# Replacing the split single-pass output product by a plain fp32 product on two row halves of the TensorE array

## The chip, the cores and the metric

The kernel runs on one core of a Trainium2 chip. The time is device microseconds of that core for one launch, as the median of several executions; the kernel before has three. A separate profiled execution supplies the trace.

## The reference

The input x has the shape (4, 4096, 512). The result is x plus two branches, both computed from the layer-normalised x. The attention branch only touches the first 16 tokens of each of the four sequences and is small. The other branch covers all 16,384 tokens and is most of the work:

```python
s = jnp.einsum('btd,dm->btm', x, Win) + bin_           # 512 -> 64
h = jax.nn.relu(s[..., None] * W1 + b1)                # 64 -> 64 x 16
g = jnp.einsum('btmh,mh->btm', h, W2) + b2             # 64 x 16 -> 64
out = jnp.einsum('btm,md->btd', g, Wout) + bout        # 64 -> 512
```

All of it is float32.

## The kernel before

The tokens are cut into N = 16 groups of 1,024. A group is loaded as eight tiles of 128 tokens, 4 MB in all with its store. The tiles b = 0 (token tiles 0 to 3) and b = 1 (4 to 7) live on two halves of the partitions: in G, partitions 0 to 63 hold the 64 values g of one half of the tokens, and partitions 64 to 127 those of the other.

The order is written out by hand. Each engine runs its own in-order program through the same slots t = 0, 1, 2, ...; a group n starts at slot 8n, and step k of it is due at slot 8n + k. Up to five groups overlap, so that once the pipeline is full every slot modulo 8 holds the same work. The steps are:

- `transpose` (L369 to L378, PE, slots 0 to 7): four 128x128 blocks of x into one PSUM bank, `T_ps[k % 2]`; for k < 2 it waits for load half k. `evacuate` (L508, ACT) copies the bank to xT.
- `s_product` (L380, PE, slots 2, 7, 8, 9): two column halves of the array, 64 columns each. `scale_s` (L765, DVE, slot 10) multiplies by the inverse standard deviation and frees the bank for the first `s_product` of the next group, which is due in the same slot (10 = 8 + 2).
- `statistics` and `variance` (L784, L790, DVE), the inverse root on POOL (L842), `spread_rstd` (PE, slot 9), `copy_rstd` (ACT).
- `s_high`, `s_low`, `replicate` (PE, slots 13 and 17), `relu` (ACT, slots 13 to 20) and `sum_h` (L413, PE, slots 19 to 22; four column tiles of 32).
- G: `g_high` (L544, ACT, slot 23) writes the rounded value g_hi and `g_low` (L776, DVE, slot 24) the rest g_lo to the other partition half, both in the float32r format. G's 128 partitions are then g_hi and g_lo of the same tokens.
- `project` (L430, PE, slots 25 to 32): per token tile two accumulating matmuls over 128 rows, with `wout_hi` and with `wout_lo`.
- `add` (L759, DVE, slots 26 to 33): residual plus product, 128x512, one a tile. `add_bias` (POOL, L867) made the residual before.
- The SP queue stores four tiles at a time once they are added, and loads a later group behind each store.

The attention branch is woven between these steps by `reach(side, ...)`, which runs the next piece of `pe_attention`, `act_attention`, `dve_attention` or `pool_attention` at half-slots of its own. It has three rounds of 24 half-slots from half-slot 34 on and ends by slot T_ATT = 56. Until then its products use one of the two product banks (`A_ps = o_ps[1]`), and `project` has the other alone.

In each slot PE runs: transpose, spread_rstd, attention, project, replicate, sum_h, s_product, attention. DVE runs: add, scale_s, s_low, g_low, attention, statistics, variance, attention.

Of the kernel before, what the change touches and what calls it, by code (L numbers as in the profile page):

```python
# [18 lines left out]
def residual_block(nc, x, Wq, bq, Wk, Wv, bv, Wo, bo, lna_w, lnc_w, lnd_w, Wlq, blq, Wlk, blk, Wlv, blv,  # L19
# [32 lines left out]
    with ctx:  # L52
# [8 lines left out]
        def sem(name):  # L61
            return ctx.enter_context(nc.semaphore(name))
# [22 lines left out]
        w2s = sb("w2s", [P, 2, HK, MH])  # L85
        wout_hi = sb("wout_hi", [P, D], F32R)
        wout_lo = sb("wout_lo", [P, D], F32R)
        bias_row = sb("bias_row", [P, D])
        ones_d = sb("ones_d", [P, P])
        T_ps, s_ps, g_ps, o_ps, rep_ps = [ps("T0"), ps("T1")], ps("s"), ps("g"), [ps("op0"), ps("op1")], ps("rep", 2)  # L90


        xa, lna = Hr[0][1][0:RW, 0:D], Hr[0][1][0:RW, D:2 * D]
        wo2, row1 = Hr[0][0][:, 0:D], Hr[0][0][:, D:2 * D]
        w_nat = [o_sb[i // 2][:, (i % 2) * DC * D:(i % 2 + 1) * DC * D].rearrange("p (c i) -> p c i", c=DC) for i in range(4)]
# [41 lines left out]
        att = vn  # L137
        A_ps = o_ps[1]
        banks = [rep_ps[:, 0:D], rep_ps[:, D:2 * D], o_ps[0][:, :]]
        NB = len(banks)  # L140
# [12 lines left out]
        relu_done, g_done = sem("relu_done"), sem("g_done")  # L153
        hi_done, lo_done = sem("hi_done"), sem("lo_done")
        op_done, xc_done, add_done = sem("op_done"), sem("xc_done"), sem("add_done")
# [9 lines left out]
        turned, turn_dve, turn_act = sem("turned"), sem("turn_dve"), sem("turn_act")  # L165
        spread_made, relu_made, w2s_made, bias_made, wout_made = (
            sem(n) for n in ("spread_made", "relu_made", "w2s_made", "bias_made", "wout_made"))
        qk_ps, qkn_made, v_ps, vn_made, qkT_ps, qkT_made, vT_ps, vT_made = (
# [30 lines left out]

        def product_bank(n, j):  # L200

            t = SLOTS * n + PROJECT + j
            return o_ps[0 if t < T_ATT else j % 2][:, :]

# [13 lines left out]
        def store(n, h):  # L218
            m = n % RING
            sp.wait_ge(add_done, SLOTS * n + 4 * (h + 1))  # L220
            c = slice(h * HALF, (h + 1) * HALF)
            sp.dma_start(out_v[n, :, c], o_sb[m][:, c]).then_inc(st[m][h], 16)

        def sp_program():
# [7 lines left out]
            sp.dma_start(wo2[0:M, :], Wout).then_inc(in_wo2, 16)  # L232
            sp.dma_start(wo2[M:P, :], Wout).then_inc(in_wo2, 16)
            sp.dma_start(bias_row[:, :], bout.partition_broadcast(P)).then_inc(in_rows, 16)
# [156 lines left out]
        def spread_rstd(n):  # L391
            pe.wait_ge(rstd_done, 2 * n + 2)
            if n > 1:
                pe.wait_ge(lo_done, 2 * (n - 1))
            for j in range(4):
                mm = pe.transpose(g_ps[:, j * P:(j + 1) * P], rwide[:, j, :, :].rearrange("p b m -> p (b m)"), ident[:, :])  # L396
            mm.then_inc(rb_done, 1)
# [15 lines left out]
        def sum_h(n, k):  # L413
            pe.wait_ge(relu_done, SLOTS * n + HK + k + 1)
            if k == 0:
                if n == 0:
                    pe.wait_ge(w2s_made, 1)
                if n == N - 1:
                    pe.wait_ge(lo_done, 2 * n)
                else:  # L420
                    pe.wait_ge(R_done, n + 2)
# [8 lines left out]
        def project(n, j):  # L430
            m, t = n % RING, SLOTS * n + PROJECT + j
            if j == 0:
                if n == 0:
                    pe.wait_ge(wout_made, 1)
                pe.wait_ge(lo_done, 2 * n + 2)
            if t >= T_ATT:
                if t <= T_ATT + 1:
                    pe.wait_ge(att_made, 1)
                pe.wait_ge(add_done, SLOTS * n + j - 1)
            elif SLOTS * n + j > 0:  # L440
                pe.wait_ge(add_done, SLOTS * n + j)
            for part in (wout_hi, wout_lo):
                mm = pe.matmul(product_bank(n, j), G[m][:, j * P:(j + 1) * P], part[:, :], start=(part is wout_hi), stop=(part is wout_lo))  # L443
            mm.then_inc(op_done, 1)

        def pe_program():
            pe.wait_ge(ident_made, 1)
            side = [0, pe_attention()]
            for t in range(SLOTS * BODIES):
# [4 lines left out]
                reach(side, 2 * t)  # L454
                if at := due(t, PROJECT, SLOTS):
                    project(*at)
# [51 lines left out]
        def evacuate(n, k):  # L508
            c, b = divmod(k, 2)
            act.wait_ge(tr_done, SLOTS * n + k + 1)  # L510
            if n > 0:
                act.wait_ge(sc_done, 4 * (n - 1) + c + 1)
            act.activation(xT[:, c, b * BLK:(b + 1) * BLK], T_ps[k % 2][:, :], ACT.Copy).then_inc(ev_done, 1)  # L513

# [14 lines left out]
        def relu(n, r):  # L529
            half, k = divmod(r, HK)  # L530
            if k == 0:
                if n == 0:
                    act.wait_ge(xn_made, 1)
                    act.wait_ge(relu_made, 1)
                    act.wait_ge(wout_made, 1)
                    act.wait_ge(bias_made, 1)
                act.wait_ge(rep_done, 2 * n + half + 1)
# [5 lines left out]

        def g_high(n):  # L544
            m = n % RING
            if n == 0:
                act.wait_ge(in_ffn, 16 * 12)
            act.wait_ge(g_done, HK * n + HK)
            for b in range(2):
                own, _, cols = halves(b)  # L550
                act.activation(G[m][own, cols], g_ps[own, :], ACT.Identity, bias=b2c[own, 0:1]).then_inc(hi_done, 1)  # L551

        def act_program():
# [12 lines left out]
            for t in range(SLOTS * BODIES):  # L566
# [6 lines left out]
                reach(side, 2 * t)  # L573
                if at := due(t, G_HIGH):
                    g_high(at[0])
                if at := due(t, RELU, 2 * HK):
# [4 lines left out]
        def dve_attention():  # L581
# [57 lines left out]
            yield 17  # L639
            dve.wait_ge(in_wo2, 32)  # L640
            v = tick(dve.tensor_copy(wout_hi[:, :], wo2))
            dve.wait_ge(in_rows, 32)
            dve.tensor_tensor(bias_row[:, :], bias_row[:, :], row1, ALU.add).then_inc(bias_made, 1)
            dve.wait_ge(dve_own, v)
            dve.tensor_tensor(wout_lo[:, :], wo2, wout_hi[:, :].bitcast(F32), ALU.subtract).then_inc(wout_made, 1)

# [129 lines left out]
        def g_low(n):  # L776
            m = n % RING
            for b in range(2):
                own, other, cols = halves(b)
                dve.wait_ge(hi_done, 2 * n + b + 1)  # L780
                dve.scalar_tensor_tensor(G[m][other, cols], g_ps[own, :], b2c[own, 0:1], G[m][own, cols].bitcast(F32),  # L781
                                         ALU.add, ALU.subtract).then_inc(lo_done, 1)

# [16 lines left out]
        def dve_program():  # L800
            side = [0, dve_attention()]
            for t in range(SLOTS * BODIES):
                if at := due(t, ADD, SLOTS):
# [5 lines left out]
                if at := due(t, G_LOW):  # L809
                    g_low(at[0])  # L810
                reach(side, 2 * t)
# [26 lines left out]
        def inv_std(n):  # L838
            pool.wait_ge(var_done, n + 1)
            if n > 0:  # L840
                pool.wait_ge(rb_done, n)
            pool.tensor_tensor(rstd[:, :], veps[:, :], nhalf[:, 0:TPP], ALU.pow).then_inc(rstd_done, 1)  # L842
            pool.wait_ge(rstd_done, 2 * n + 1)
            pool.tensor_tensor(rwide[:, :, :, :], rstd[:, :].rearrange("p (b j) -> p j b", b=2).unsqueeze(3)
                               .to_broadcast([P, TPP // 2, 2, M]),
# [120 lines left out]
```

## Time and profile before

| | |
|---|---|
| median of 3 runs | 374.67 us (374.19 to 376.34) |
| the profiled execution's own time | 375.8 us |
| its span in the trace | 373.7 us |
| PE busy | 337.0 us (90%) |
| DVE, ACT, POOL busy | 282.9, 278.2, 237.3 us (76, 74, 64%) |

The span is what the trace shows between the first and the last instruction; 2.1 us of the execution's own time lie around it. Busy time of PE comes from matmul records that overlap, so the distance between starts tells more than the durations.

### The profile page before, as it was taken

What the parts mean: (1) busy time and instruction counts of PE and PEld (TensorE: products, weight loads), DVE (VectorE), ACT (ScalarE), POOL (GpSimd) and SP (SyncE); (2) the same over time, 40 slices, a digit from 0 to 9 for tenths busy, and PEclk for the clock granted to TensorE, in tenths of its full rate; (3) what the DMA queues carried; (4) which work ended last, traced back from release to release, by engine and by line L of the source; (5) the groups of instructions that cost most, each with busy time, mean ns of one, the idle gap of its engine ahead of it and who ended that gap; (6) DMA issues with size and microseconds to landing.
All of it is one profiled execution on the core that took longest, in us unless ns stands there. A gap on an engine that the chain in (4) does not pass through costs nothing.

```text
span 373.7 us, 5638 instructions
## 1 busy us (share of the span) xinstructions
PE 337.0 (90%) x1964; PEld 161.1 (43%) x1964; DVE 282.9 (76%) x507; ACT 278.2 (74%) x366; POOL 237.3 (64%) x209
## 2 busy tenths in 40 slices
PE   2489889789997998898999999999999999999774
PEld 2274554345533553444444444444434444443322
DVE  0677757888788799987969687877878787877664
ACT  0363568785786677867998999998989898988820
POOL 8405385992767649839094949494949585769900
PEclk9999989999999999999999999999999999999998
DMA  8999303334346425653575757576756652223647
GB/s 254 266 383 348 117 3 113 112 114 125 157 168 227 153 100 198 224 170 128 216 275 205 263 205 269 203 260 224 280 211 249 224 224 114 113 114 140 208 157 296
DMA packets 15052, 73.02 MB, mean 195 GB/s; under 512 B 4121, under 2 KB 4273, under 8 KB 6833
## 3 DMA queue, kind: packets, MB, share of 16 engines
q1 hardware_dynamic: 12304, 72.23, 53.1%
q0 software_dynamic: 640, 0.16, 0.8%
q10 hardware_dynamic: 2080, 0.28, 0.8%
q8 instruction: 16, 0.26, 0.3%
q14 instruction: 12, 0.09, 0.1%
HBM read 38.96 MB, written 33.69 MB: 194 GB/s over the span
## 4 chain that ended last, share of the span: by engine, by line
PE 63%; POOL 10%; DVE 8%; ACT 6%; issue 5%; DMA 5%; SPq 1%; POOLq 0%; DVEq 0%; ACTq 0%
PE op L443 14%; PE T L377 14%; PE g L425 13%; PE s L387 12%; POOL o L867 7%; DMA o<-in_L_attn_Wv_dram 5%; PE rep L410 4%; ACT H L541 3%; DVE stats L788 2%; PE g L396 1%; POOL rstd L842 1%; DVE o L763 1%; ACT G L551 1%; PE op L276 1%; DVE SH L774 1%
## 5 line engine op out<-in xcount | busy, mean ns | idle before, releaser
L867 POOL TENSOR_TENSOR o<-x,bias_row 128x512 f32<-128x512 f32 x128 | 164.1, 1319 | 4.0 <-issue 4.0
L541 ACT ACTIVATE H<-rep,b1c,w1c 128x1024 f32<-128x1024 f32 x128 | 153.6, 1206 | 14.5 <-PE rep L410 13.7
L763 DVE TENSOR_TENSOR o<-o,op 128x512 f32<-128x512 f32 x128 | 86.9, 682 | 39.3 <-PE op L443 38.3
L513 ACT ACTIVATE xT<-T 128x512 f32<-128x512 f32 x128 | 76.2, 596 | 39.7 <-PE T L377 39.2
L377 PEld LDWEIGHTS T<-ident,x 128*128 128x128 f32 x512 | 54.9, 142 | 107.4 <-issue 75.9
L377 PE MATMUL T<-ident,x 128*128 128x128 f32 x512 | 84.9, 289 | 11.6 <-DMA x<-in_L_attn_x_dram 9.1
L788 DVE BATCH_NORM_STATS2 stats<-x 128x6 f32<-128x512 f32 x128 | 83.2, 682 | 0.4
L842 POOL TENSOR_TENSOR rstd<-veps,nhalf 128x8 f32<-128x8 f32 x16 | 26.4, 1651 | 83.9 <-DVE veps L798 83.9
L387 PE MATMUL s<-xT,win 128*64 128x512 f32 x256 | 70.5, 630 | 0.0
L425 PE MATMUL g<-H,w2s 128*32 128x512 f32 x512 | 68.2, 605 | 0.4 <-ACT H L541 0.4
L443 PE MATMUL op<-wout_hi,G 128*128 128x512 f32 x128 | 62.7, 490 | 5.9 <-DVE G L781 3.7
L443 PE MATMUL op<-wout_lo,G 128*128 128x512 f32 x128 | 51.5, 403 | 0.0
L443 PEld LDWEIGHTS op<-wout_hi,G 128*128 128x128 f32 x128 | 24.5, 192 | 21.1 <-DVE o L763 13.6
L443 PEld LDWEIGHTS op<-wout_lo,G 128*128 128x128 f32 x128 | 24.9, 195 | 0.3
L781 DVE SCALAR_TENSOR_TENSOR G<-g,b2c,G 64x512 fp32r<-64x512 f32 x32 | 24.0, 749 | 1.1
L774 DVE TENSOR_TENSOR SH<-s_full,SH 64x512 fp32r<-64x512 f32 x32 | 23.3, 728 | 2.0 <-ACT SH L527 1.0
L551 ACT ACTIVATE G<-g,b2c 64x512 fp32r<-64x512 f32 x32 | 21.7, 678 | 3.7 <-PE g L425 3.3
L387 PEld LDWEIGHTS s<-xT,win 128*64 128x64 f32 x256 | 13.0, 137 | 22.1 <-issue 18.7
L410 PE MATMUL rep<-SH,spread 128*128 128x512 f32 x64 | 21.5, 417 | 0.7 <-ACT H L541 0.5
L768 DVE TENSOR_TENSOR s_full<-s,s_full 128x512 f32<-128x512 f32 x16 | 11.1, 692 | 14.4 <-PE s L387 14.4
L527 ACT ACTIVATE SH<-s_full 64x512 fp32r<-64x512 f32 x32 | 20.0, 625 | 0.4
L425 PEld LDWEIGHTS g<-H,w2s 128*32 128x32 f32 x512 | 10.1, 108 | 23.1 <-issue 21.5
(166 smaller groups left out, 246.5 us busy)
## 6 DMA issues: line engine op xcount, KB each, us to landing
x<-in_L_attn_x_dram SPq DMA_DIRECT2D x32, 1024.0 KB, 6.8
out_dram<-o SPq DMA_DIRECT2D x32, 1024.0 KB, 4.3
o<-in_L_attn_Wq_dram SPq DMA_DIRECT2D x1, 1024.0 KB, 14.6
o<-in_L_attn_Wk_dram SPq DMA_DIRECT2D x1, 1024.0 KB, 16.4
o<-in_L_attn_Wv_dram SPq DMA_DIRECT2D x1, 1024.0 KB, 19.4
o<-in_L_attn_Wo_dram SPq DMA_DIRECT2D x1, 1024.0 KB, 19.2
H<-in_L_ffn_Wout_dram SPq DMA_DIRECT2D x2, 128.0 KB, 14.7
bias_row<-in_L_ffn_bout_dram SPq DMA_DIRECT2D x1, 256.0 KB, 12.1
```

The costliest lines, as they stand in the source:

```text
L377: mm = pe.transpose(T_ps[k % 2][:, j * P:(j + 1) * P], x_sb[m][:, col0:col0 + P], ident[:, :])
L387: mm = pe.matmul(s_ps[b * M:(b + 1) * M, :], win[:, c, :], xT[:, c, b * BLK:(b + 1) * BLK], start=(c == 0), stop=(c == DC - 1))
L410: mm = pe.matmul(rep_ps[:, cols], spread[:, half, :], SH[:, cols], start=True, stop=True)
L425: mm = pe.matmul(g_ps[at0:at0 + MH, :], w2s[:, half, k, :], Hr[half][k % len(Hr[half])][:, b * BLK:(b + 1) * BLK], start=(k == 0), stop=(k ...
L443: mm = pe.matmul(product_bank(n, j), G[m][:, j * P:(j + 1) * P], part[:, :], start=(part is wout_hi), stop=(part is wout_lo))
L513: act.activation(xT[:, c, b * BLK:(b + 1) * BLK], T_ps[k % 2][:, :], ACT.Copy).then_inc(ev_done, 1)
L541: act.activation(Hr[half][k % len(Hr[half])][:, :], rep_ps[:, :], ACT.Relu, bias=b1c[:, half, k:k + 1], scale=w1c[:, half, k:k + 1]).then_ ...
L763: dve.tensor_tensor(o_sb[m][:, c], o_sb[m][:, c], product_bank(n, j), ALU.add).then_inc(add_done, 1)
L774: dve.tensor_tensor(SH[other, cols], s_full[own, :], SH[own, cols].bitcast(F32), ALU.subtract).then_inc(sl_done, 1)
L788: dve.bn_stats(stats[:, j, :], x_sb[m][:, j * D:(j + 1) * D]).then_inc(bn_done, 1)
L842: pool.tensor_tensor(rstd[:, :], veps[:, :], nhalf[:, 0:TPP], ALU.pow).then_inc(rstd_done, 1)
L867: pool.tensor_tensor(o_sb[m][:, c], x_sb[m][:, c], bias_row[:, :], ALU.add).then_inc(xc_done, 1)
```

## The change

G is kept as one plain fp32 tile for each group: `evacuate_g` (ACT, slot 23) writes all 128 partitions in one instruction, `g_low` and the split of Wout go. `project` runs every other slot (25, 27, 29, 31) for a pair of token tiles, one from each half: two fp32 matmuls over 64 rows each, at row positions 0 and 64 of the array, into the two banks of `o_ps`. One `add` for each pair covers 128x1024, and it is due in the slot of its own project. For the pair to be neighbours in the output, tile 2j + b takes the place of tile 4b + j, so that every transpose needs both halves of a load: both are waited for at k = 0. Since both product banks are taken, the attention's products move to `T_ps[1]`, and until slot T_ATT all transposes go through `T_ps[0]`, each waiting for the copy of the one before it.

```diff
-        G = [sb(f"G{r}", [P, PAIR], F32R) for r in range(RING)]
+        G = [sb(f"G{r}", [P, BLK]) for r in range(2)]
-        REPLICATE, RELU, SUM_H, G_HIGH, G_LOW, PROJECT, ADD, BIAS = (13, 17), 13, 19, 23, 24, 25, 26, 10
+        REPLICATE, RELU, SUM_H, G_MADE, PROJECT, ADD, BIAS = (13, 17), 13, 19, 23, 25, 25, 10
+        TILES = TPP // 2
+        def turn_bank(n, k):
+
+            return T_ps[0 if SLOTS * n + k < T_ATT else k % 2]
+
+        def every_other(t, first):
+
+            at = due(t, first, SLOTS)
+            return (at[0], at[1] // 2) if at and at[1] % 2 == 0 else None
...
-            if k < 2:
-                pe.wait_ge(ld[m][k], 16 * (n // RING + 1))
-            if SLOTS * n + k > 1:
-                pe.wait_ge(ev_done, SLOTS * n + k - 1)
-            for j in range(4):
-                col0 = (4 * b + j) * D + c * P
-                mm = pe.transpose(T_ps[k % 2][:, j * P:(j + 1) * P], x_sb[m][:, col0:col0 + P], ident[:, :])
+            if k == 0:
+                for h in range(2):
+                    pe.wait_ge(ld[m][h], 16 * (n // RING + 1))
+            t = SLOTS * n + k
+            if 0 < t <= T_ATT:
+                pe.wait_ge(ev_done, t)
+            elif t == T_ATT + 1:
+                pe.wait_ge(att_made, 1)
+            elif t > 0:
+                pe.wait_ge(ev_done, t - 1)
+            for j in range(TILES):
+                col0 = (2 * j + b) * D + c * P
+                mm = pe.transpose(turn_bank(n, k)[:, j * P:(j + 1) * P], x_sb[m][:, col0:col0 + P], ident[:, :])
...
-            for part in (wout_hi, wout_lo):
-                mm = pe.matmul(product_bank(n, j), G[m][:, j * P:(j + 1) * P], part[:, :], start=(part is wout_hi), stop=(part is wout_lo))
+            if TILES * n + j > 0:
+                pe.wait_ge(add_done, TILES * n + j)
+            for b in range(2):
+                own = slice(b * M, (b + 1) * M)
+                mm = pe.matmul(o_ps[:, b * D:(b + 1) * D], G[n % 2][own, j * P:(j + 1) * P], wout[own, :],
+                               start=True, stop=True, tile_position=(b * M, 0))
...
-            for b in range(2):
-                own, _, cols = halves(b)
-                act.activation(G[m][own, cols], g_ps[own, :], ACT.Identity, bias=b2c[own, 0:1]).then_inc(hi_done, 1)
+            act.activation(G[n % 2][:, :], g_ps[:, :], ACT.Identity, bias=b2c[:, 0:1]).then_inc(g_made, 1)
...
-            m, c = n % RING, slice(j * D, (j + 1) * D)
-            dve.wait_ge(op_done, SLOTS * n + j + 1)
-            dve.wait_ge(xc_done, SLOTS * n + j + 1)
-            dve.tensor_tensor(o_sb[m][:, c], o_sb[m][:, c], product_bank(n, j), ALU.add).then_inc(add_done, 1)
+            m, c = n % RING, slice(2 * j * D, (2 * j + 2) * D)
+            dve.wait_ge(op_done, TILES * n + j + 1)
+            dve.wait_ge(xc_done, SLOTS * n + 2 * j + 2)
+            dve.tensor_tensor(o_sb[m][:, c], o_sb[m][:, c], o_ps[:, :], ALU.add).then_inc(add_done, 1)
```

## Rows read from the trace of the kernel before

**Rows 1.** The page: busy time, share of the span, instructions of each engine.

```profile
PE 337.0 (90%) x1964; PEld 161.1 (43%) x1964; DVE 282.9 (76%) x507; ACT 278.2 (74%) x366; POOL 237.3 (64%) x209
```

**Rows 2.** Windows: busy time of each engine in a stretch, clock, DMA share, GB/s.

```profile
200.00:250.00 50.00, 50.00 (x295) 22.48 (x292) 38.89 (x70) 45.58 (x59) 34.83 (x28) 1.00 0.63 231
```

**Rows 3.** Timeline, slots 1 and 2 of a full period: start, duration, engine, line.

```profile
192.88 1.28 DVE L788 BATCH_NORM_STATS2 stats<-x 128x6 f32<-128x512 f32 x2
...
193.80 0.48 PE L443 MATMUL op<-wout_hi,G 128*128 128x512 f32 x1
...
194.35 0.64 PE L410 MATMUL rep<-SH,spread 128*128 128x512 f32 x2
194.54 0.69 DVE L763 TENSOR_TENSOR o<-o,op 128x512 f32<-128x512 f32 x1 [0.39 <-PE op L443]
...
194.92 1.08 PE L387 MATMUL s<-xT,win 128*64 128x512 f32 x4
...
195.93 0.66 PE L377 MATMUL T<-ident,x 128*128 128x128 f32 x4
196.04 0.69 DVE L768 TENSOR_TENSOR s_full<-s,s_full 128x512 f32<-128x512 f32 x1 [0.81 <-PE s L387]
196.34 0.48 PE L443 MATMUL op<-wout_hi,G 128*128 128x512 f32 x1
...
196.98 1.08 PE L387 MATMUL s<-xT,win 128*64 128x512 f32 x4
...
214.90 1.08 PE L387 MATMUL s<-xT,win 128*64 128x512 f32 x4
```

**Rows 4.** Timeline: transposes followed by work without a project between.

```profile
57.95 0.66 PE L377 MATMUL T<-ident,x 128*128 128x128 f32 x4
...
58.44 0.60 PE L318 MATMUL op<-kT,bd 128*128 128x256 f32 x2
...
70.21 0.66 PE L377 MATMUL T<-ident,x 128*128 128x128 f32 x4
70.79 1.08 PE L387 MATMUL s<-xT,win 128*64 128x512 f32 x4
```

**Rows 5.** Timeline: eight plain fp32 matmuls in a row on two column halves.

```profile
34.34 3.65 PE L276 MATMUL op<-o,xnT 128*64 128x512 f32 x16
37.82 1.03 PE L387 MATMUL s<-xT,win 128*64 128x512 f32 x4
```

**Rows 6.** The page's groups: weight loads and the add; mean ns before the bar.

```profile
L763 DVE TENSOR_TENSOR o<-o,op 128x512 f32<-128x512 f32 x128 | 86.9, 682 | 39.3 <-PE op L443 38.3
...
L443 PEld LDWEIGHTS op<-wout_hi,G 128*128 128x128 f32 x128 | 24.5, 192 | 21.1 <-DVE o L763 13.6
...
L387 PEld LDWEIGHTS s<-xT,win 128*64 128x64 f32 x256 | 13.0, 137 | 22.1 <-issue 18.7
```

**Rows 7.** Timeline of the start.

```profile
6.77 1.09 PE L377 MATMUL T<-ident,x 128*128 128x128 f32 x4 [6.77 <-DMA x<-in_L_attn_x_dram]
...
9.49 0.22 DVE L593 TENSOR_SCALAR wmean<-g 128x64 f32<-128x64 f32 x1 [9.49 <-PE g L251]
...
11.83 1.12 PE L377 MATMUL T<-ident,x 128*128 128x128 f32 x4 [2.38 <-DMA x<-in_L_attn_x_dram]
...
24.98 0.66 PE L270 MATMUL op<-ident,o 128*128 128x128 f32 x4 [0.57 <-DMA o<-in_L_attn_Wv_dram]
```

**Rows 8.** Timeline: attention work on DVE and the PE product behind it.

```profile
106.49 1.22 DVE L716 TENSOR_TENSOR WvT<-qk,hmask 128x1024 f32<-128x1024 f32 x1
...
107.63 1.37 DVE L722 TENSOR_SCALAR qk<-qk,wq_it 128x256 f32<-128x256 f32 x1
...
109.05 1.08 PE L342 MATMUL op<-WvT,qk 128*64 128x256 f32 x8 [0.27 <-DVE qk L722]
```

**Rows 9.** Timeline of the tail: the last projects.

```profile
359.02 0.50 PE L443 MATMUL op<-wout_hi,G 128*128 128x512 f32 x1
...
362.10 0.49 PE L443 MATMUL op<-wout_hi,G 128*128 128x512 f32 x1 [1.87 <-DVE G L781]
```

More of the change, by code:

```diff
@@ L85, in residual_block @@
         w2s = sb("w2s", [P, 2, HK, MH])
-        wout_hi = sb("wout_hi", [P, D], F32R)
-        wout_lo = sb("wout_lo", [P, D], F32R)
+        wout = sb("wout", [P, D])
         bias_row = sb("bias_row", [P, D])
         ones_d = sb("ones_d", [P, P])
-        T_ps, s_ps, g_ps, o_ps, rep_ps = [ps("T0"), ps("T1")], ps("s"), ps("g"), [ps("op0"), ps("op1")], ps("rep", 2)
+        T_ps, s_ps, g_ps, o_ps, rep_ps = [ps("T0"), ps("T1")], ps("s"), ps("g"), ps("op", 2), ps("rep", 2)
         xa, lna = Hr[0][1][0:RW, 0:D], Hr[0][1][0:RW, D:2 * D]
-        wo2, row1 = Hr[0][0][:, 0:D], Hr[0][0][:, D:2 * D]
+        row1 = Hr[0][0][:, 0:D]
         w_nat = [o_sb[i // 2][:, (i % 2) * DC * D:(i % 2 + 1) * DC * D].rearrange("p (c i) -> p c i", c=DC) for i in range(4)]
@@ L137, in residual_block @@
         att = vn
-        A_ps = o_ps[1]
-        banks = [rep_ps[:, 0:D], rep_ps[:, D:2 * D], o_ps[0][:, :]]
+        A_ps = T_ps[1]
+        banks = [rep_ps[:, 0:D], rep_ps[:, D:2 * D], o_ps[:, 0:D], o_ps[:, D:2 * D]]
         NB = len(banks)
@@ L153, in residual_block @@
         relu_done, g_done = sem("relu_done"), sem("g_done")
-        hi_done, lo_done = sem("hi_done"), sem("lo_done")
+        g_made = sem("g_made")
         op_done, xc_done, add_done = sem("op_done"), sem("xc_done"), sem("add_done")
@@ L165, in residual_block @@
         turned, turn_dve, turn_act = sem("turned"), sem("turn_dve"), sem("turn_act")
-        spread_made, relu_made, w2s_made, bias_made, wout_made = (
-            sem(n) for n in ("spread_made", "relu_made", "w2s_made", "bias_made", "wout_made"))
+        spread_made, relu_made, w2s_made, bias_made = (
+            sem(n) for n in ("spread_made", "relu_made", "w2s_made", "bias_made"))
         qk_ps, qkn_made, v_ps, vn_made, qkT_ps, qkT_made, vT_ps, vT_made = (
@@ L219, in store @@
             m = n % RING
-            sp.wait_ge(add_done, SLOTS * n + 4 * (h + 1))
+            sp.wait_ge(add_done, TILES * n + 2 * (h + 1))
             c = slice(h * HALF, (h + 1) * HALF)
@@ L231, in sp_program @@
                     load(n, h)
-            sp.dma_start(wo2[0:M, :], Wout).then_inc(in_wo2, 16)
-            sp.dma_start(wo2[M:P, :], Wout).then_inc(in_wo2, 16)
+            sp.dma_start(wout[0:M, :], Wout).then_inc(in_wo2, 16)
+            sp.dma_start(wout[M:P, :], Wout).then_inc(in_wo2, 16)
             sp.dma_start(bias_row[:, :], bout.partition_broadcast(P)).then_inc(in_rows, 16)
@@ L393, in spread_rstd @@
             if n > 1:
-                pe.wait_ge(lo_done, 2 * (n - 1))
-            for j in range(4):
+                pe.wait_ge(g_made, n - 1)
+            for j in range(TILES):
                 mm = pe.transpose(g_ps[:, j * P:(j + 1) * P], rwide[:, j, :, :].rearrange("p b m -> p (b m)"), ident[:, :])
@@ L418, in sum_h @@
                 if n == N - 1:
-                    pe.wait_ge(lo_done, 2 * n)
+                    pe.wait_ge(g_made, n)
                 else:
@@ L454, in pe_program @@
                 reach(side, 2 * t)
-                if at := due(t, PROJECT, SLOTS):
+                if at := every_other(t, PROJECT):
                     project(*at)
@@ L512, in evacuate @@
                 act.wait_ge(sc_done, 4 * (n - 1) + c + 1)
-            act.activation(xT[:, c, b * BLK:(b + 1) * BLK], T_ps[k % 2][:, :], ACT.Copy).then_inc(ev_done, 1)
+            act.activation(xT[:, c, b * BLK:(b + 1) * BLK], turn_bank(n, k)[:, :], ACT.Copy).then_inc(ev_done, 1)
         def copy_rstd(n):
@@ L542, in relu, with evacuate_g @@
                            bias=b1c[:, half, k:k + 1], scale=w1c[:, half, k:k + 1]).then_inc(relu_done, 1)
-        def g_high(n):
-            m = n % RING
+        def evacuate_g(n):
             if n == 0:
@@ L573, in act_program @@
                 reach(side, 2 * t)
-                if at := due(t, G_HIGH):
-                    g_high(at[0])
+                if at := due(t, G_MADE):
+                    evacuate_g(at[0])
                 if at := due(t, RELU, 2 * HK):
@@ L774, in s_low @@
                 dve.tensor_tensor(SH[other, cols], s_full[own, :], SH[own, cols].bitcast(F32), ALU.subtract).then_inc(sl_done, 1)
[L776 to L782, printed above, removed]
         def statistics(n, j):
@@ L802, in dve_program @@
             for t in range(SLOTS * BODIES):
-                if at := due(t, ADD, SLOTS):
+                if at := every_other(t, ADD):
                     add(*at)
@@ L808, in dve_program @@
                     s_low(at[0])
-                if at := due(t, G_LOW):
-                    g_low(at[0])
                 reach(side, 2 * t)
@@ L843, in inv_std @@
             pool.wait_ge(rstd_done, 2 * n + 1)
-            pool.tensor_tensor(rwide[:, :, :, :], rstd[:, :].rearrange("p (b j) -> p j b", b=2).unsqueeze(3)
+            pool.tensor_tensor(rwide[:, :, :, :], rstd[:, :].rearrange("p (j b) -> p j b", b=2).unsqueeze(3)
                                .to_broadcast([P, TPP // 2, 2, M]),
```

20 lines of the change are left out of this document (3 added, 17 removed).

## The prediction, made before the changed kernel ran

> **What bounds the kernel now.** I read the page first: PE is busy 90% of the span, DVE, ACT and POOL 76, 74 and 64% [rows 1]. The windows say where it binds: from 200 to 250 us PE has no idle time at the full clock, while ACT has 45.6 of 50 and DVE 38.9 [rows 2]. The timeline of that stretch gives the measure: the same s product starts at 196.98 and at 214.90, so eight slots take 17.92 us [rows 3]. The trace is in three parts: the attention phase up to about 172 us, where PE is nearly full but also waits for the attention's chain; about nine such periods up to 335 us, set by PE; and a tail. The sum is made on the profiled span, 373.7 us; its execution took 375.8, 0.3% over the median of 374.67, so I add the difference to the median. No change within 0.5% can be told by such a measurement.
>
> **PE in a full period, before.** Start to start [rows 3]: project to the next s or g product 0.64; project to replicate 0.55; s product to transposes 1.01; transposes to project 0.41. So a slot without replicate spends 1.05 from transposes to the product that follows. The plain fp32 product has a unit in the trace: 16 records on two column halves take 37.82 - 34.34 = 3.48 us [rows 5], that is 0.435 for one pass of 512 columns, with both halves running at once. A lone pair of halves takes 1.01, so starting and draining cost 0.14 beside its two passes.
>
> **The new project.** Two fp32 matmuls on row halves. No row of this trace has row halves. Bounds: if both run at once like the column halves, 1.01 plus the longer weight load, 192 against 137 ns [rows 6], gives 1.06 us a pair; if they run one after the other, two more passes, 1.93. With weight loads and drains hidden it is 0.87. I take 1.06, the row of the nearest kind. What it stands in for is 2 x 0.64.
>
> **The neighbours pay too.** Transposes followed by a product of the same tiling start it 0.49 later (57.95 to 58.44), by one on column halves 0.58 later (70.21 to 70.79), and by today's project 0.41 [rows 3, 4]. The project now acts as a buffer: transposes hand over to it cheaply, its own 0.64 holds the change to column tiles. Without it the slot pays 0.58. The Trainium skill, TensorEngine Tiling (Array Packing), Key Properties, says that changing the tiling mode drains the array; the 0.09 between 0.49 and 0.58 agrees for column tiles, and no row shows it for row tiles. By that rule both sides of the new project pay; without it the sum would be that of the first rival.
>
> Sum over eight slots. Slots 0, 2, 4, 6 lose the project: 1.05 becomes 0.58, -0.47 each, -1.88. Slots 3 and 7: 1.05 becomes 0.58 + 1.06, +0.59 each, +1.18. Slots 1 and 5, where replicate follows: the project's 0.55 becomes 1.06 + 0.11 (replicate's weights no longer load under it) and the entry costs 0.17 more, +0.79 each, +1.58. Together +0.88 us a period: the product itself gets a little cheaper, the array's changes eat it.
>
> **A wait that the change adds.** DVE is in order. Today the add of a tile is due one slot after its project; now the add is due in the project's own slot, so everything behind it on DVE waits for PE. In slot 1 that is: add, two statistics, and in slot 2 scale_s, which frees the PSUM bank for the next s product, also due in slot 2. Let E be the moment at which PE is done with the project of slot 1. The add starts at E + 0.10 (194.54 against 193.80 + 0.64), takes 1.25 (bounds: 1.22 for a 1024-wide operation of DVE [rows 8], 2 x 0.68 [rows 6]), two statistics 1.28, scale_s 0.69 [rows 3]: E + 3.32. PE wants the bank after replicate 0.11 + 0.57, s product 1.01, transposes 0.58: E + 2.27. It stands still 1.05 us, once a period, and s products, transposes, and with them ACT, stand behind it. Today scale_s ends at 196.73 and the s product starts at 196.98, a slack of 0.25 [rows 3]; the statistics ran before the add. In slots 3 to 5 the same reckoning for s_low leaves some 0.2 us of slack, so no second wait.
> Full periods: 9 x (0.88 + 1.05) = +17.4 us. Bounds: 0.87 products with hidden loads give about -0.6 in place of +0.88 and the wait remains, +4; one after the other, 4 x 0.87 more a period, +49.
>
> **The start.** The first transposes need one load half, at 6.77; now both, and the second lands at 11.83 [rows 7]. PE is in order, so the column sums of Win behind them, and with these DVE's first operation at 9.49, move by 5.06; the layer norm of the attention's tokens is queued behind it on DVE. What absorbs it: PE's own idle before the Wv weights at 24.98 (0.57) [rows 7], and smaller waits on the way. I take +3, between 0 and +5. Waiting for both halves costs later groups nothing: they are loaded slots ahead.
>
> **The attention phase.** 16 pairs at 0.22 a pair, 3.5, of which I count 3 because PE also waits here. The late add strikes three kinds of place: slot 2 of a period as above (slots 26, 34, 50: 1.0, 0.5, 1.0, the middle one under another wait); DVE's attention work at slots 29 and 41, behind add and statistics, which PE wants in the next slot (1.8 and 1.1); and at 35 and 47 the pair L716, L722 of 1.2 and 1.3 us behind the add: PE waits 0.27 for it today [rows 8], tomorrow some 2.5 more. Together 10.4. Credits: in even slots there is no add before attention work (-0.68 at four or five places on the chain), project no longer shares one bank with the add of the tile before, ACT writes G in one instruction in place of two: -5 in all. Net +8.5, between +2 and +14. The single transpose bank costs nothing visible: the copy of slot t - 1 stands first on ACT, and is done before PE comes to slot t; the price if not is one copy, 0.6 a slot.
>
> **The tail.** Removed: the second half of G's copy and g_low, part of the 3.08 us between 359.02 and 362.10 [rows 9]. Added: the last four pairs take turns with their adds over one buffer, 4 x (1.06 + 1.25 + 0.1). They cancel: 0, between -1.5 and +3. DMA and POOL do the same work, POOL's bias adds in another order at most.
>
> **Sum.** 3 + 8.5 + 17.4 + 0 = +28.9: span 402.6, median 374.67 + 28.9 = 403.6 us.
>
> **Rivals.** (1) Going between full rows and row halves costs nothing: loads hide, the pair takes 0.87. PE's sum is then about -0.6 a period, but the wait on scale_s remains: 9 x 0.45 + 3 + 5 = +12 to +19, 387 to 394. For it: today's project loads its weights under the transposes. Against: the 0.09 and 0.14 of the column halves.
> (2) The halves run one after the other. No row excludes it. +0.87 on 52 pairs beside other work, 45 us: about 448. The Trainium skill, TensorE: Matmul & The Clock Gate, Measured speedup vs the span model, has row tiles run together within some ns each; by it this rival falls, and the trace shows togetherness for column halves alone.
> (3) Faster: a pair takes one pass, 0.43 in place of 1.06 (both passes of both halves at once, no drain). 64 x 0.63 = 40 us less than forecast, some of it not usable in the tail: about 368. It decides from a pair below 0.58 on, where 52 pairs and the neighbours pay for the added waits. Against it: two passes of 0.435 in every fp32 product here.
> (4) No change: DVE's waits vanish under others and the switches too; only the start remains, within 2 us of before. Against: the slack of 0.25 at scale_s.
>
> **Chances.** Forecast (396 to 412) 0.60; rival 1 0.18, with 0.03 for what lies between it and no change; rival 2 0.09; rival 3 0.06; rival 4 0.04. Faster by over 0.5%: 0.06, within: 0.04, slower: 0.90. The range takes the forecast and rival 1, 386 to 414, and leaves out the one-after-the-other case and the faster ones.
>
> **What would show it.** Right: the period 19.8 us in the middle; project records of both halves starting together, pairs 1.06 from start to what follows; transposes to s or g product 0.58 in even slots; a wait of the first s product for scale_s of about 1 us each period; DVE's first operation near 14.5. Wrong: a period under 18.5, pairs near 1.9, or no idle PE in the middle. What would make the number wrong although the steps hold: waits in the attention phase that overlap more than I count.

## The result, and the profile after

The changed kernel takes 378.52 us (median of 20 executions), the kernel before 375.61 in the same series: ratio 1.0072, with a 95% interval of 1.0051 to 1.0093. It is slower, by 2.9 us: less than one per cent, but the interval leaves out equal times. I had predicted 403.6 us with a range of 386 to 414. The direction was right; the size was ten times too large.

Most of the miss has its reason in the section ahead of the prediction, and it is a plain misreading. The changed kernel has PROJECT at 24 and ADD at 25. I wrote and reckoned with 25 and 25; the excerpt of the diff above repeats the error in that one line, and so does the sentence about slots 25, 27, 29, 31 and the add in the slot of its own project. In the kernel that ran, the pairs stand in the even slots 24, 26, 28, 30, and each add is due one slot after its project. The line is

```diff
-        REPLICATE, RELU, SUM_H, G_HIGH, G_LOW, PROJECT, ADD, BIAS = (13, 17), 13, 19, 23, 24, 25, 26, 10
+        REPLICATE, RELU, SUM_H, G_MADE, PROJECT, ADD, BIAS = (13, 17), 13, 19, 23, 24, 25, 10
```

The page of the changed kernel, busy times and the granted clock in 40 slices of the span:

```profile
PE 338.2 (90%) x1964; PEld 142.8 (38%) x1964; DVE 245.8 (65%) x409; ACT 265.7 (70%) x350; POOL 234.9 (62%) x209
...
PEclk9999989999999999999999999999999999999965
```

DVE lost 37 us of work and ACT 12.5; PE has as much as before [rows 1]. The clock digits fall to 6 and 5 at the very end. A window of its middle, with the columns of [rows 2]:

```profile
200.00:250.00 50.00, 50.00 (x283) 18.98 (x280) 31.98 (x52) 42.40 (x55) 36.35 (x30) 1.00 0.61 225
```

The middle is still PE's: it has no idle time there, at the full clock. The timeline of one period there, from slot 1 on:

```profile
190.19 0.66 PE L387 MATMUL T<-ident,x 128*128 128x128 f32 x4
190.69 0.60 PE L406 MATMUL g<-ident,rwide 128*128 128x128 f32 x4
191.04 0.70 PE L420 MATMUL rep<-SH,spread 128*128 128x512 f32 x2
191.68 1.08 PE L397 MATMUL s<-xT,win 128*64 128x512 f32 x4
192.69 0.66 PE L387 MATMUL T<-ident,x 128*128 128x128 f32 x4
193.27 1.13 PE L450 MATMUL op<-wout,G 64*128 64x512 f32 x4
194.33 1.08 PE L397 MATMUL s<-xT,win 128*64 128x512 f32 x4
195.34 0.66 PE L387 MATMUL T<-ident,x 128*128 128x128 f32 x4
...
208.51 0.66 PE L387 MATMUL T<-ident,x 128*128 128x128 f32 x4
```

A pair takes 194.33 - 193.27 = 1.06 us, the price forecast. From transposes to the pair it is 0.58. Slot 1 has no project, and transposes, spread_rstd and replicate follow each other at 0.50 and 0.35. The period is 208.51 - 190.19 = 18.32, against 17.92 [rows 3].

The same transposes mark how the two executions run apart. Slots 24 and 56 of the kernel before, and of the changed kernel:

```profile
74.67 0.55 PE L377 MATMUL T<-ident,x 128*128 128x128 f32 x3
...
172.98 0.44 PE L377 MATMUL T<-ident,x 128*128 128x128 f32 x2
```

```profile
76.53 0.55 PE L387 MATMUL T<-ident,x 128*128 128x128 f32 x3
...
169.22 0.55 PE L387 MATMUL T<-ident,x 128*128 128x128 f32 x3
```

The last transposes (slot 127) start at 332.16 and 332.45. So the 3.4 us between the spans of these two profiled executions (377.1 and 373.7) is a sum of four terms:

| stretch | before | after | difference |
|---|---|---|---|
| start, to slot 24 | 74.67 | 76.53 | +1.86 |
| attention phase, slots 24 to 56 | 98.31 | 92.69 | -5.62 |
| full periods, slots 56 to 127 | 159.18 | 163.23 | +4.05 |
| tail, to the end of the span | 41.5 | 44.65 | +3.1 |

The middle two terms repeat well: the profiled executions of four of the kernels below that leave these stretches alone give 92.68 to 92.71 and 163.22 to 163.29. The first one does not. Slot 24 comes between 75.73 and 77.82 in the nine profiled kernels with the changed kernel's order at the start, and at 74.67 and 74.80 in the two with the old one, so the start costs between 0.9 and 3.2 us.

The start, in the timeline after: the first transposes and DVE's first operation.

```profile
11.76 1.09 PE L387 MATMUL T<-ident,x 128*128 128x128 f32 x4 [11.76 <-DMA x<-in_L_attn_x_dram]
...
14.48 0.23 DVE L597 TENSOR_SCALAR wmean<-g 128x64 f32<-128x64 f32 x1 [14.48 <-PE g L255]
```

Both are 5 us later than in [rows 7], as forecast. The tail after, its last three pairs and adds:

```profile
360.83 1.22 DVE L763 TENSOR_TENSOR o<-o,op 128x1024 f32<-128x1024 f32 x1 [1.71 <-PE op L450]
362.11 2.08 PE L450 MATMUL op<-wout,G 64*128 64x512 f32 x4 [1.32 <-DVE o L763]
364.24 1.22 DVE L763 TENSOR_TENSOR o<-o,op 128x1024 f32<-128x1024 f32 x1 [2.18 <-PE op L450]
365.51 2.08 PE L450 MATMUL op<-wout,G 64*128 64x512 f32 x4 [1.32 <-DVE o L763]
...
371.04 1.22 DVE L763 TENSOR_TENSOR o<-o,op 128x1024 f32<-128x1024 f32 x1 [2.18 <-PE op L450]
```

Pair and add wait for each other in turn (1.32 and 2.18 us), and the pairs are twice as long as in the middle, at half the clock, as the window shows:

```profile
362.00:372.30 10.30, 6.23 (x12) 1.51 (x12) 3.72 (x4) 0.00 (x0) 0.00 (x0) 0.50 0.29 118
```

The kernel before is not free of this: its clock stands at 0.50 from 363.2 to 366.6 us, under three of its last projects. There the stretch ends before the work does.

### The profile page after: what moved, and what is told of

The parts are those of the page before. It is cut to its first block, busy times and chain, and to the rows that moved or that the text cites. A ratio compares the mean times of both kernels' runs of the same rounds, so it can differ in the third digit from the quotient of the medians.

```text
span 377.1 us, 5444 instructions
## 1 busy us (share of the span) xinstructions
PE 338.2 (90%) x1964; PEld 142.8 (38%) x1964; DVE 245.8 (65%) x409; ACT 265.7 (70%) x350; POOL 234.9 (62%) x209
## 4 chain that ended last, share of the span: by engine, by line
PE 74%; ACT 9%; DVE 9%; issue 3%; DMA 3%; POOL 0%; SPq 0%; ACTq 0%; DVEq 0%
PE op L450 17%; PE T L387 16%; PE g L435 14%; PE s L397 14%; ACT H L548 5%; PE rep L420 3%; DMA x<-in_L_attn_x_dram 3%; DVE o L763 2%; PE g L406 2%; DVE stats L780 1%; ACT SH L535 1%; PE T L280 1%; DVE WvT L716 1%; PE T L346 1%; PE op L274 1%
## 5 line engine op out<-in xcount | busy, mean ns | idle before, releaser
L857 POOL TENSOR_TENSOR o<-x,bias_row 128x512 f32<-128x512 f32 x128 | 161.6, 1300 | 2.9 <-PE T L387 2.9
L763 DVE TENSOR_TENSOR o<-o,op 128x1024 f32<-128x1024 f32 x64 | 78.0, 1218 | 65.8 <-PE op L450 65.7
L450 PE MATMUL op<-wout,G 64*128 64x512 f32 x256 | 75.1, 664 | 6.2 <-DVE o L763 4.3
L450 PEld LDWEIGHTS op<-wout,G 64*128 64x128 f32 x256 | 19.9, 190 | 26.1 <-DVE o L763 11.8
L420 PE MATMUL rep<-SH,spread 128*128 128x512 f32 x64 | 23.1, 441 | 1.9 <-ACT H L548 1.1
L834 POOL TENSOR_TENSOR rwide<-rstd,ones_d 128x512 f32<-128x512 f32 x16 | 17.0, 1061 | 1.3
L823 POOL TENSOR_TENSOR rstd<-var,nhalf 128x16 f32<-128x16 f32 x3 | 8.8, 2935 | 13.1 <-ACT var L498 13.1
L555 ACT ACTIVATE G<-g,b2c 128x512 f32<-128x512 f32 x16 | 10.9, 683 | 3.7 <-PE g L435 3.7
L420 PEld LDWEIGHTS rep<-SH,spread 128*128 128x128 f32 x64 | 9.9, 191 | 3.8 <-ACT H L548 1.9
```

The source lines that it names most:

```text
L420: mm = pe.matmul(rep_ps[:, cols], spread[:, half, :], SH[:, cols], start=True, stop=True)
L450: mm = pe.matmul(o_ps[:, b * D:(b + 1) * D], G[n % 2][own, j * P:(j + 1) * P], wout[own, :], start=True, stop=True, tile_position=(b * M, 0))
L763: dve.tensor_tensor(o_sb[m][:, c], o_sb[m][:, c], o_ps[:, :], ALU.add).then_inc(add_done, 1)
L857: pool.tensor_tensor(o_sb[m][:, c], x_sb[m][:, c], bias_row[:, :], ALU.add).then_inc(xc_done, 1)
```

## The experiments

Eleven kernels ran. Times are medians; ratios are to the kernel before in the same series, with 95% intervals.

**The kernel that I had predicted.** Edit of the changed kernel:

```diff
-        REPLICATE, RELU, SUM_H, G_MADE, PROJECT, ADD, BIAS = (13, 17), 13, 19, 23, 24, 25, 10
+        REPLICATE, RELU, SUM_H, G_MADE, PROJECT, ADD, BIAS = (13, 17), 13, 19, 23, 25, 25, 10
```

> The changed kernel with PROJECT and ADD both at 25, the placement for which the prediction was worked out. The theory that its price list is right: PE +0.9 us a period over the kernel before and a wait of the first s product for scale_s of about 1 us each period, a period near 19.8 us, some 390 to 404 us in all. The rival, that the late add costs little because DVE has room: a period near 18.8 and 381 to 386 us.

Measured: 406.45 us, ratio 1.0824 (1.0791 to 1.0857). Its timeline, DVE and PE from slot 4 through slots 1 and 2 to the next slot 4:

```profile
234.73 0.66 PE L387 MATMUL T<-ident,x 128*128 128x128 f32 x4
...
247.66 1.22 DVE L763 TENSOR_TENSOR o<-o,op 128x1024 f32<-128x1024 f32 x1 [3.47 <-PE op L450]
...
249.99 0.68 DVE L768 TENSOR_TENSOR s_full<-s,s_full 128x512 f32<-128x512 f32 x1
...
250.81 1.08 PE L397 MATMUL s<-xT,win 128*64 128x512 f32 x4 [0.94 <-DVE s_full L768]
...
254.46 0.66 PE L387 MATMUL T<-ident,x 128*128 128x128 f32 x4
```

The period is 254.46 - 234.73 = 19.73 (reckoned: 19.85) and PE waits 0.94 us in it for scale_s (reckoned: 1.05). The time is 0.7% above the 403.6 of the prediction. Its slots 24, 56 and 127 come at 77.47, 184.68 and 359.57 us, so against the kernel before the start costs 2.8 us (forecast 3), the attention phase 8.9 (8.5), the full periods 15.7 (17.4) and the tail 3.4 (0). Some 1.7 us of the 8.9, by an estimate, are luck: a stretch of 3.4 us at half clock from 157.5 us on, which the kernel before does not have in this phase. But for the tail, the working held for the kernel it described; that kernel was not the one on the table.

**The pairs in odd slots, the add one later.** PROJECT, ADD = 25, 26.

> The changed kernel with PROJECT at 25 and ADD at 26: the pairs move from even to odd slots, where two of the four stand before replicate, and the add keeps its one slot of distance. Theory that the switches between array tilings set the price: the period goes from 18.32 to about 18.8 us, 4 to 6 us slower than the changed kernel, with no wait for scale_s. Rival, that only the pair itself costs and its neighbours do not: the same time within 1 us.

Measured: 395.01 us, ratio 1.0519 (1.0483 to 1.0555). Timeline of PE:

```profile
188.34 0.66 PE L387 MATMUL T<-ident,x 128*128 128x128 f32 x4
...
202.82 0.66 PE L387 MATMUL T<-ident,x 128*128 128x128 f32 x4
203.78 1.08 PE L397 MATMUL s<-xT,win 128*64 128x512 f32 x4 [0.30 <-DVE s_full L768]
...
207.43 0.66 PE L387 MATMUL T<-ident,x 128*128 128x128 f32 x4
```

The period is 19.09. In slot 2 the s product starts 0.96 after the transposes instead of 0.58, which I had not expected: the add of slot 1's pair now stands directly ahead of scale_s, and PE waits for scale_s. Without that 0.38 the period is 18.71, against the 18.8 of the price list. So the parity of the slots is worth 0.4 us a period on PE, as the recorded theory says. The total is another matter: 16.5 us over the changed kernel, where 4 to 6 were expected and the periods explain 9 x 0.77 = 7. By slot 56 this kernel is already 9.2 us behind. By an estimate, 1.7 us of that come from a stretch at half clock (0.52 from 173.5 to 177 us); the rest was not taken apart.

**The price of the pair.**

```diff
-            for b in range(2):
+            for b in (0, 1, 0, 1):
```

> The changed kernel with each pair of matmuls issued twice into the same banks, the second overwriting the first with the same values. It measures the pair by itself: the period grows by four times the price of two passes without a switch of tiling. If both halves run at once, 4 x 0.87 = +3.5 us a period, and some +45 to +50 us in all, 425 to 430; if the halves run one after the other, 4 x 1.74 = +7.0 us a period.

Measured in a single execution: 431.73 us. Timeline of PE:

```profile
300.87 1.99 PE L450 MATMUL op<-wout,G 64*128 64x512 f32 x8
302.79 1.08 PE L397 MATMUL s<-xT,win 128*64 128x512 f32 x4
```

Two pairs take 302.79 - 300.87 = 1.92, so the second adds 0.86, twice the 0.435 of one pass [rows 5]: the halves run at once. The transposes of slots 96 and 104 are 316.03 - 294.27 = 21.76 apart, +3.44 over the changed kernel's period, for 3.5 expected. The other 0.20 of a pair's 1.06 is spent once, before or behind the passes; a weight load that nothing covers and a change of tiling are both in it, and no run parts them. The Trainium skill, TensorEngine Tiling (Array Packing), Key Properties, says that a change of tiling mode drains the array; the trace is in line with it for row tiles too, with 0.58 us from transposes to the pair where work in the same tiling starts after 0.49 [rows 4] or 0.50 (190.19 to 190.69).

**The product on row halves, or the pairing?** The changed kernel's banks, pairs and adds, with the split product of before: for each of the two tiles,

```diff
-                mm = pe.matmul(o_ps[:, b * D:(b + 1) * D], G[n % 2][own, j * P:(j + 1) * P], wout[own, :],
-                               start=True, stop=True, tile_position=(b * M, 0))
+                for part in (wout_hi, wout_lo):
+                    mm = pe.matmul(o_ps[:, b * D:(b + 1) * D], G[n % RING][:, c0:c0 + P], part[:, :],
+                                   start=(part is wout_hi), stop=(part is wout_lo))
```

with g_high, g_low and PROJECT, ADD = 26, 27 (c0 is the tile's first column in G).

> The changed kernel's banks, pairs, token order and 128x1024 adds, but with the split product of the kernel before: G as high and low part, four full-row matmuls for a pair, in slots 26, 28, 30, 32. It tells pairing from the product on row halves. Theory that the longer period is the price of the row halves and their change of tiling: a period of 17.9 us as before, 3 to 4 us less than the changed kernel in the middle, 373 to 375 in all with the same start and a tail like its own. Rival, that pairing itself (an empty slot, then a full one) makes the period longer: 18.2 to 18.5 us.

Measured: 385.71 us, ratio 1.0226 (1.019 to 1.0263), where 373 to 375 us were expected. Timeline of PE:

```profile
189.92 0.66 PE L388 MATMUL T<-ident,x 128*128 128x128 f32 x4
190.41 0.60 PE L407 MATMUL g<-ident,rwide 128*128 128x128 f32 x4
191.24 0.74 PE L421 MATMUL rep<-SH,spread 128*128 128x512 f32 x2 [0.22 <-ACT H L551]
...
208.31 0.66 PE L388 MATMUL T<-ident,x 128*128 128x128 f32 x4
```

The period is 18.39, which is the number of the recorded rival (18.2 to 18.5), but not for its reason: replicate starts 0.83 after spread_rstd instead of 0.35, because it waits for relu on ACT. Without these 0.48 us PE's work would be 17.91. The slots themselves bear this out. A slot without a pair takes 1.6 us in both kernels; a slot with one takes 2.52 here, from one group of transposes to the next,

```profile
192.92 0.66 PE L388 MATMUL T<-ident,x 128*128 128x128 f32 x4
...
195.44 0.66 PE L388 MATMUL T<-ident,x 128*128 128x128 f32 x4
```

and 195.34 - 192.69 = 2.65 in the changed kernel. So once two tiles are taken together, the split product adds 0.93 to a slot and the row halves add 1.06: PE's longer period in the changed kernel is the row halves' price, and the pairing alone costs nothing on PE. That the wait for relu comes from G's two instructions on ACT is likely, but no run isolates it. Part of the rest of the loss is in the tail, where g_low stands ahead of the last pairs and these again take turns with their adds at the half clock: 48.9 us behind slot 127, against 44.65.

**The attention phase: banks, ACT, DVE.** The gain of 5.62 us between slots 24 and 56 was the largest unexplained term. First the banks alone, on the kernel before:

```diff
-        A_ps = o_ps[1]
+        A_ps = T_ps[1]
...
-            t = SLOTS * n + PROJECT + j
-            return o_ps[0 if t < T_ATT else j % 2][:, :]
+            return o_ps[j % 2][:, :]
```

with the single transpose bank and the waits of the change.

> The kernel before, with only the PSUM banks of the change: the attention's products in T_ps[1], transposes through T_ps[0] alone until slot 56, and project alternating two product banks from the start. Theory that the changed kernel's gain of 5 us in the attention phase comes from the product bank, which is no longer single there: 3 to 5 us faster than before, about 371, with the steady period unchanged at 17.92. Rival, that it comes from the relief of DVE and ACT (no second half of G, half as many adds): no change, or slightly slower for the single transpose bank, 375 to 377.

Measured: 372.32 us, ratio 0.9919 (0.9888 to 0.995): faster than both kernels. Slots 24 and 56 in its timeline:

```profile
74.80 0.44 PE L385 MATMUL T<-ident,x 128*128 128x128 f32 x2
...
170.29 0.55 PE L385 MATMUL T<-ident,x 128*128 128x128 f32 x3
```

95.49 against 98.31, a gain of 2.82 us: half of the term. This execution has a stretch at half clock in the phase, which neither the kernel before nor the changed one has there:

```profile
120.50:123.50 3.00, 3.00 (x22) 1.46 (x20) 1.92 (x3) 1.03 (x3) 3.00 (x3) 0.50 0.23 96
```

By an estimate from it, 3 us of work at half speed, the banks may be worth 1.5 us more than the 2.82.

The kernel with pairs and split product, above, takes the next step from here. It has the changed kernel's banks, pairs and 128x1024 adds, and yet ACT's two instructions and DVE's g_low as before the change:

```profile
76.72 0.44 PE L388 MATMUL T<-ident,x 128*128 128x128 f32 x2
...
169.51 0.44 PE L388 MATMUL T<-ident,x 128*128 128x128 f32 x2
```

Its slots 24 to 56 take 92.79, against 92.69 in the changed kernel. So the term falls into 2.82 for the banks, 2.70 for the pairs with half as many adds (95.49 to 92.79; less by what the half clock took from the banks), and 0.10 for the last step, from the split product to the row halves. That last one is small because two things meet in it: the row halves are dearer, 16 pairs at 0.13 us, and G takes less work on ACT and DVE. The next two kernels price this work.

On the changed kernel, ACT's step was made as long as before:

```diff
-            act.activation(G[n % 2][:, :], g_ps[:, :], ACT.Identity, bias=b2c[:, 0:1]).then_inc(g_made, 1)
+            for b in range(2):
+                own, _, _ = halves(b)
+                act.activation(G[n % 2][own, :], g_ps[own, :], ACT.Identity, bias=b2c[own, 0:1]).then_inc(g_made, 1)
```

> The changed kernel with G written by ACT in two instructions of 64 partitions, as before the change, 1.38 us in place of 0.68 once a group. Theory that ACT's shorter step is part of the gain in the attention phase: 1 to 2 us slower by slot 56. Rival, that ACT has slack there and in the full periods: within 0.7 us of the changed kernel, and at most 1 us more in the tail, where ACT sets the pace.

Measured: 387.1 us, ratio 1.03 (1.0252 to 1.0349). Slots 24 and 56, and between them and the last row the place of a new wait:

```profile
77.82 0.55 PE L387 MATMUL T<-ident,x 128*128 128x128 f32 x3
...
172.16 0.44 PE L387 MATMUL T<-ident,x 128*128 128x128 f32 x2
...
209.22 0.66 PE L387 MATMUL T<-ident,x 128*128 128x128 f32 x4
210.24 1.13 PE L450 MATMUL op<-wout,G 64*128 64x512 f32 x4 [0.36 <-ACT G L557]
```

Slots 24 to 56 take 94.34, +1.65 over the changed kernel. The full periods, where the rival had allowed nothing, grow to 18.76: the first pair of a group is due one slot after G and now starts 1.02 after its transposes instead of 0.58. With G a slot ahead of the pair, the one ACT instruction in place of two is worth 0.44 us a full period. In the attention phase the wait is another one. The second G instruction stands ahead of the attention's own work on ACT, and PE waits for that in slots 32 and 40, which take 0.82 and 0.84 us more. The whole is 8.6 us longer than the changed kernel.

Then DVE, with two operations of 64x512 at slot 24, in g_low's place:

```diff
+            for b in range(2):
+                own, other, cols = halves(b)
+                dve.scalar_tensor_tensor(idle[other, :], G[n % 2][own, :], b2c[own, 0:1], G[n % 2][own, :], ALU.add, ALU.subtract)
```

> The changed kernel with two 64x512 operations on DVE at slot 24 of each group (into a scratch tile that nobody reads), as long as the removed g_low, about 1.5 us. Theory that the part of the attention phase's gain that the banks do not explain, some 3 us, comes from DVE's relief: 2 to 3 us slower than the changed kernel, all of it before slot 56, the period still 18.3. Rival, that it comes from project's even slots or from ACT: within 0.7 us of the changed kernel.

Measured: 381.72 us, ratio 1.0146 (1.0112 to 1.018). Slots 24 and 56:

```profile
76.76 0.44 PE L388 MATMUL T<-ident,x 128*128 128x128 f32 x2
...
170.30 0.55 PE L388 MATMUL T<-ident,x 128*128 128x128 f32 x3
```

93.54, +0.85, with the period unchanged. Less than the 2 to 3 us expected. Of the 2.6 us between the spans (379.7 and 377.1) 1.5 lie behind slot 127, in the tail. ACT's 1.65 and DVE's 0.85 together are 2.5 us, and the row halves' price of 16 x 0.13 = 2.1, an estimate, takes most of it back: this is the last step of 0.10. That the two shares add up is an inference. So the gain of 5.62 us is the banks' and the pairs'; it would have come without the row halves, in this phase.

**The start.** On PE, `reach(side, 0)` ahead of the loop, so that the column sums of Win precede the first transposes.

> The changed kernel with the column sums of Win issued on PE ahead of the first transposes, so that DVE's first chain does not wait for the second load half. Theory that the late start is carried into the attention phase: slot 32 comes 1 to 2 us earlier and the whole is 1 to 2 us faster than the changed kernel, 376.5 to 377.5. Rival, that the attention phase has slack for it: the same time within 0.5 us.

Measured: 374.65 us, ratio 0.9983 (0.9957 to 1.0008), against the changed kernel's 1.0072: some 3 us, more than expected. The windows of 30 to 60 us of the changed kernel and of this one:

```profile
30.00:60.00 30.00, 27.55 (x155) 14.85 (x153) 19.56 (x62) 16.52 (x25) 17.30 (x14) 0.94 0.36 127
```

```profile
30.00:60.00 30.00, 28.11 (x166) 15.13 (x168) 22.41 (x62) 19.08 (x29) 17.02 (x14) 1.00 0.43 151
```

Slot 12 comes at 43.19 instead of 45.57, 2.4 us earlier, and slot 16 at 50.73 instead of 54.73, 4.0 earlier: 1.6 us are a stretch of half clock near 50 us. The profiled executions of the changed kernel and of the kernel before both have it (clock 0.94 in this window), and this one has not. That difference belongs to the execution: of the nine profiled kernels with the changed kernel's start, four have the stretch and five have not. Those five lose about as much earlier, as in this line of the two-buffer kernel below:

```profile
22.65 1.11 PE L393 MATMUL T<-ident,x 128*128 128x128 f32 x4
```

Four transposes take 1.11 us there, the time of the half clock, although the clock column still reads 1.00; the changed kernel's at 22.43 take 0.66. What the order itself gives is seen before this: slot 3 comes at 20.04 and 20.27 us in the two kernels with the sums first, and at 21.62 to 22.67 in the nine others, so 1.4 to 2.6 us. At slot 24 they are 72.52 and 72.99 against 75.73 to 77.82.

**The tail.** Two buffers for the last eleven pairs (the transpose banks are free after slot 127):

```diff
+        def pair_bank(n, j):
+
+            q = TILES * n + j
+            return T_all if SLOTS * n + PROJECT + 2 * j > SLOTS * N and q % 2 else o_ps
```

> The changed kernel, whose last eleven pairs, after the last transpose, alternate between the product banks and the two transpose banks. Theory that the tail loses its 3 us because pair and add take turns over one buffer: the last four pairs, now 3.4 us apart, come 1.3 to 2.1 us apart, 3 to 6 us off the changed kernel, 373 to 376. Rival, that the tail is set by relu and sum_h before them: at most 1 us.

Measured: 372.63 us, ratio 0.9908 (0.9879 to 0.9937). The last two pairs:

```profile
364.24 1.13 PE L460 MATMUL op<-wout,G 64*128 64x512 f32 x4 [0.46 <-DVE o L773]
365.37 1.13 PE L460 MATMUL T<-wout,G 64*128 64x512 f32 x4
```

They are 1.1 us apart instead of 3.4, and at the full clock. Its clock is not full throughout: it reads 0.50 from 352 to 355 us. To part clock from turn-taking, the other kernel keeps one buffer and fills the gaps with work that nobody reads:

```diff
+            if n == N - 1 and j > 0:
...
+                for _ in range(2):
+                    for b in range(2):
+                        own = slice(b * M, (b + 1) * M)
+                        pe.matmul(T_ps[b][:, 0:D // 2], G[n % 2][own, 0:P], wout[own, 0:D // 2],
+                                  start=True, stop=True, tile_position=(b * M, 0))
```

> The changed kernel with TensorE kept at work in the last three gaps: before each of the last three pairs it runs two throwaway pairs of 256 columns on the same operands into the idle transpose banks. Buffers and waits stay. Theory that a large part of the tail's loss is the granted clock, which falls to 0.5 at 362 us and doubles the pairs from 1.06 to 2.1 us: pairs back at 1.1, 3 us less, 375 to 376. Rival, that only the turn-taking counts or that the filling comes too late to hold the clock: no gain, or up to 1 us lost.

Measured: 376.21 us, ratio 0.9982 (0.9955 to 1.0009). Its window over the last pairs:

```profile
362.00:369.00 7.00, 4.45 (x28) 2.02 (x24) 3.67 (x3) 0.00 (x0) 0.00 (x0) 1.00 0.37 152
```

The clock stays at 1.00. The last two intervals between pairs are 2.45 us (363.79 to 366.24) instead of 3.40, and the last pair takes 1.1 instead of 2.1: 2.9 us. The whole gains as much: 0.9982 against 1.0072. So the clock alone is worth about 3 us in these pairs, and two buffers spare it in them together with the turn-taking.

**Both repairs.**

> The changed kernel with both repairs: the column sums first and two buffers for the last eleven pairs. If start and tail are separate terms, as the chain says, their gains of 4 and some 5 us add up: about 370 us, faster than the kernel before by 1.5%. If the time gained at the start is lost again in the tail (stores queued, relu setting the pace), 372 to 374.

Measured: 368.51 us, ratio 0.9801 (0.9765 to 0.9836), 2% faster than the kernel before and the fastest of all. Its profiled execution has no low stretch while TensorE works:

```profile
PEclk9999999999999999999999999999999999999999
```

## Why the prediction was wrong, point by point

- The step that failed is "now the add is due in the project's own slot", and with it "slots 1 and 5, where replicate follows". With the true constants the same prices, and 0.35 and 0.41 read from the changed kernel for what follows transposes or spread_rstd directly, give for eight slots: four slots with a pair, 1.05 to 1.64, +2.36; slots 3 and 7, -0.94; slots 1 and 5 without project, 0.91 to 0.35 and 0.96 to 0.41, -1.11. That is +0.31 us a period where I had +0.88; measured +0.40. And no wait for scale_s, where I had +1.05: in the add's true slot the full periods cost 4.05 us in place of 17.4. The kernel that has these constants as I read them took 406.45 us, against 403.6, with the tail's miss and a shorter sum over the periods partly cancelling.
- The pair at 1.06 us: right to the hundredth; both halves at once: right. What it replaces was priced at 2 x 0.64 = 1.28, the price of two tiles in slots of their own. Taken together they cost 0.93, as the kernel with pairs and split product shows, so the product did not get cheaper by the row halves.
- The neighbours pay: right in size, 0.58 to the pair and 0.20 beside its passes. That it is the change of tiling, and not an uncovered weight load, is argued.
- The start, +3: measured +1.86 up to slot 24 in this pair of executions, 0.9 to 3.2 over all, in the range; 1.4 to 2.6 us return when PE's queue is reordered.
- The attention phase, +8.5: measured -5.6. The 10.4 us of waits behind the late add fall with the misreading. What was left of my reckoning, +3 for PE and -5 of credits, was still 3.6 us too little gain: the step that failed here is the term "-5 in all". Its "project no longer shares one bank with the add of the tile before" is worth 2.8 us or more alone, the pairs with half as many adds another 2.7 or less, and "ACT writes G in one instruction in place of two" 1.65.
- The tail, 0: measured +3.1. The step that failed is the term "4 x (1.06 + 1.25 + 0.1)". The turns were there, but behind a stretch of waits the granted clock fell to 0.50, and a pair took 2.1.
- None of the rivals describes this kernel. Rival 4, no change, at a chance of 0.04, came nearest, though not by its mechanism: the four terms of the table nearly cancel.

## What to carry to other kernels

Copy a schedule's constants from the diff by position before reckoning with them, and redo the count of what shares each slot: one slot of distance between a product and the add behind it was worth 11 us here (406.45 to 395.01), and moving both together by one slot another 16, of which about half stays unexplained. Price an array product together with what stands before and after it, and compare like with like: two split products one behind the other add 0.93 us to a slot, and the pair of row halves 1.06. Look at the two ends by themselves: a queue order at the start and a single buffer with a falling clock at the end cost more than the whole change, and repairing both turned 0.7% slower into 2% faster.

## What the runs showed of the hardware that was not expected

In the changed kernel the granted clock fell to 0.50, the 1.2 GHz level, just before 362 us and stayed there for its last three pairs. PE had been busy for 16.0 of the 21 us before, with no single wait above 1.3 us. In the profiled executions with two buffers or throwaway work it read 1.00, the 2.4 GHz level, under the last pairs. Closing the gaps gives no warrant, though: with two buffers it was at 0.50 from 352 to 355 us. Stretches of some 3.3 us at half clock also appear near 50 us in some executions and not in others, of kernels with the same work there; slot 15 then takes 4.75 us in place of 3.14. Among the nine executions with the same start, the five without the stretch had been slower before 30 us; the one shown above had transposes at half speed for longer, where the clock column read 1.00. Plain fp32 products on two row halves ran side by side as those on column halves do, 0.43 us for one pass of both.
